# One layer kernel: keys laid out in runs of four, expert weights in one transfer, and loads moved in the fill and the drain

## The reference, cut to what matters

```
xn   = layernorm(x)
cq, ckv, kr0 = xn@Wc+bc, xn@Wckv+bckv, xn@Wkr+bkr        # 128, 128, 256 wide
q    = [cq@Wcq+bcq , cq@Wqr+bqr]  per head               # 16 heads, 32 + 16 wide
k    = [ckv@Wck+bck, kr0]         per head ; v = ckv@Wv+bv
attn = softmax over the 16 heads of one token (q_i . k_j), then attn @ v
x    = x + layernorm(attn_out@Wo + bo)
xf   = layernorm(x)
scores = softmax(xf@gate.T) ; top 6 of 64 experts, up to 128 rows each
routed = sum over chosen experts of  (silu(g)*u)@down * weight ; [g,u] = xf@gate_up[e]   # 192 each
shared = (silu(xf@G.T) * (xf@U.T)) @ D.T                 # 384 wide
x    = x + layernorm(routed + shared)
```

## Time and profile before

| what | us |
| --- | --- |
| median of 3 runs | 1913.72 (1912.94 to 1927.52) |
| the profiled execution's own time | 1907.77 |
| its span, first to last instruction | 1906.0 |
| tokens, start to about | 1325 |
| experts, about | 1330 to 1715 |
| norm, about | 1715 to 1906 |

### The profile page before, as it was taken

One profiled execution on the slowest core, in us unless ns is written; L12 is line 12 of the kernel. 1 busy time (PEld: TensorE's weight loads), 2 busy tenths in 40 slices (PEclk: granted clock), 3 DMA queues, 4 the chain that ended last, 5 costly groups with the idle time before them and its releaser, 6 DMA issues. The chain is left out here.

```text
span 1906.0 us, 48898 instructions
## 1 busy us (share of the span) xinstructions
PE 1769.8 (93%) x14281; PEld 1418.7 (74%) x14281; DVE 1509.3 (79%) x3940; ACT 967.3 (51%) x2129; POOL 522.6 (27%) x773
## 2 busy tenths in 40 slices
PE   5799999999999999999999999965999999998986
PEld 4688888888888888888888888854545555556865
DVE  6699999999999999999999999964444445437977
ACT  4465666666666656565656565631222323323433
POOL 1021211212121212121212121111344444444767
PEclk8799999999999999999999999977999999999998
DMA  6356565656666665656665666565799999988996
GB/s 223 89 140 174 146 177 147 173 154 166 161 160 168 157 171 153 175 152 174 153 173 154 174 153 176 133 160 168 235 312 324 336 330 346 349 258 320 416 414 265
DMA packets 549276, 400.83 MB, mean 210 GB/s; under 512 B 424872, under 2 KB 433192, under 8 KB 549160
## 3 DMA queue, kind: packets, MB, share of 16 engines
q1 hardware_dynamic: 528672, 341.77, 60.0%
q0 software_dynamic: 14336, 35.66, 7.7%
q10 hardware_dynamic: 6208, 22.68, 3.2%
HBM read 249.24 MB, written 150.63 MB: 210 GB/s over the span
## 5 line engine op out<-in xcount | busy, mean ns | idle before, releaser
L942 POOL TENSOR_SCALAR ve<-mv 128x1 f32<-128x1 f32 x192 | 42.3, 220 | 920.3 <-DVE mv L759 920.3
L646 ACT COPY kT<-bank 48x256 f32<-48x256 f32 x384 | 231.4, 603 | 37.2 <-PE bank L465 29.4
L1158 PE MATMUL e_gu<-w,xgT 128*128 128x384 f32 x512 | 187.6, 511 | 12.0 <-DMA w<-w_ed 9.8
L646 ACT COPY qT<-bank 48x256 f32<-48x256 f32 x512 | 188.5, 368 | 12.9 <-PE bank L465 2.0
L472 PE MATMUL bank<-wgu,xfT 128*128 128x416 f32 x512 | 188.8, 369 | 5.9 <-ACT xfT L646 4.9
L473 PE MATMUL bank<-wgu,xfT 128*128 128x416 f32 x512 | 183.6, 359 | 0.0
L1323 DVE SCALAR_TENSOR_TENSOR tanh<-tanh,e_gu 128x192 f32<-128x192 f32 x64 | 22.7, 355 | 165.0 <-ACT tanh L1246 165.0
L1158 PEld LDWEIGHTS e_gu<-w,xgT 128*128 128x128 f32 x512 | 94.5, 194 | 70.5 <-issue 10.7
L1424 POOL DMA_INDIRECT acc_scratch<-eo,sidx x64 | 101.5, 1587 | 120.0 <-ACT eo L1242 102.9
L1181 PE MATMUL e_ps<-w,hidT 96*128 96x512 f32 x256 | 128.2, 624 | 1.5 <-ACT hidT L1234 0.9
L476 PE MATMUL bank<-wgu,xfT 128*128 128x416 f32 x512 | 120.8, 359 | 0.3 <-DVE xfT L768 0.3
(11 more groups left out here) (184 smaller groups left out, 4750.4 us busy)
## 6 DMA issues: line engine op xcount, KB each, us to landing
w<-w_eg SPq DMA_DIRECT2D x60, 768.0 KB
acc_scratch<-zero SPq DMA_DIRECT2D x130, 256.0 KB, 4.0
w<-w_ed SPq DMA_DIRECT2D x60, 384.0 KB
w<-acc_scratch SPq DMA_DIRECT2D x40, 512.0 KB, 14.5
xf_scratch<-xf SPq DMA_DIRECT2D x64, 288.0 KB, 2.1
xin<-x SPq DMA_DIRECT2D x64, 256.0 KB, 2.8
x_raw<-xt SPq DMA_DIRECT2D x64, 256.0 KB, 3.2
v_scratch<-v SPq DMA_DIRECT2D x64, 256.0 KB, 3.5
```

Source lines behind the costliest of these rows:

```text
L646: nc.scalar.copy(dst, src).then_inc(done.sem, 1)
L1158: last = nc.tensor.matmul(gu_ps[par], xgT[:, par, n, :], w1[:, place, n, :], start=(n == 0), stop=(n == KD - 1))
```

## The change

- Keys: `kT` gets the layout of `qT` (`p c h t`), all 8 copies for it are ACT's, DVE's 2 are gone with their semaphore. The scores' columns now run head by head, so `prob` is laid out `n h t`, and DVE's two maxima read the scores with a step of 4 elements (`by_key`). The order of `v` in its DRAM copy follows: 4 stores in pieces of 128 bytes take the place of one, and SP issues them right behind the next tile's inputs.
- Fill: the low parts of `wo` and of the first two parts of `wgu` (parts 7 to 12) are POOL's; four bias loads go one iteration earlier.
- SP and the drain: the accumulators are cleared three iterations earlier (`i-2`), the bulk of the ranks is read back at iteration 64, the first experts' weights are issued in iterations 66 and 67.
- Experts: an expert's weights are one array of 128 rows by 2304 elements, in one transfer. The down product's first 128 features are a full product, cut in two halves of 256 columns; the other 64 features stand on partitions 0 to 63 and, again, on 64 to 127, and each half of the columns takes one of them. For that the hidden rows have 256 columns, of which the last 64 are written by a second DVE instruction. Gathered and hidden rows are turned from contiguous columns. The two small matmuls that find rows are one.

```diff
-        kT = kT_all[:, 0:P // 2 * H].rearrange("p (t h) -> p t h", h=H)
-        prob = sb("prob", [P, NBLK, B4, H])
+        kT = kT_all[:, 0:P // 2 * H].rearrange("p (c h t) -> p c h t", h=H, t=B4)
+        prob = sb("prob", [P, NBLK, H, B4])
...
+                if active(i - 1):
+                    sp.wait_ge(d_v.sem, d_v.at(i - 1))
+                    sp.wait_ge(v_in[1 - par].sem, v_in[1 - par].at(i - 3))
+                    settle(sp)
+                    dst = v_d[1 - par].rearrange("c (j t d) -> t c j d", t=B4, d=DH)
+                    for n in range(B4):
+                        sp.dma_start(dst[n], v[n:P:B4, :].rearrange("p (j d) -> p j d", d=DH)).then_inc(v_out.sem, 16)
...
-                if active(i - 5):
+                if active(i - 2):
                     for a in acc_d:
-                        sp.dma_start(rows(a, i - 5), zero[:, 0:D]).then_inc(acc_out.sem, 16)
+                        sp.dma_start(rows(a, i - 2), zero[:, 0:D]).then_inc(acc_out.sem, 16)
...
-                    sp.dma_start(v_d[1 - par], v[:]).then_inc(v_out.sem, 16)
...
-                if isinstance(i, int) and i == NT + 2:
+                if isinstance(i, int) and i == NT:
...
                     pe.wait_ge(a_kT.sem, a_kT.at(i - 2))
-                    pe.wait_ge(d_kT.sem, d_kT.at(i - 2))
...
-                    spread(by_token, b3, a_kT, 1, (0,))
+                    spread(kT, b3, a_kT, 1)
...
+                if isinstance(i, int) and i == NT + 2:
+                    act.wait_ge(pe_k.sem, pe_k.at(NT - 1))
+                    settle(act)
+                    for n in range(2):
+                        load_expert(act, n, n)
...
+                if isinstance(i, int) and i == NT + 3:
+                    for n in range(2, NW):
+                        load_expert(act, n, n)
...
-                if isinstance(i, int) and 0 <= i - NT - 1 < 2:
-                    act.wait_ge(pe_k.sem, pe_k.at(NT - 1))
-                    settle(act)
-                    for e in range(2):
-                        load_expert(act, 2 * (i - NT - 1) + e, 2 * (i - NT - 1) + e)
...
-                    for half in range(2):
-                        nc.vector.tensor_copy(by_token[64 * half:64 * half + DQ, 1, 4:8], sv[:, half]).then_inc(d_kT.sem, 1)
...
+                by_key = score_ps[:].rearrange("p (n h t) -> p n t h", n=NBLK, t=B4)
...
-                    nc.vector.tensor_reduce(smax4[:, halves[0]], sp4[:, halves[0]], AX.X, ALU.max).then_inc(d_s.sem, 1)
+                    nc.vector.tensor_reduce(smax4[:, halves[0]], by_key[:, halves[0]], AX.X, ALU.max).then_inc(d_s.sem, 1)
...
-                    pool.wait_ge(part_lo, 11)
+                    for n in ON_POOL:
+                        stage, w, m, _ = parts[n]
+                        pool.wait_ge(part_hi, n + 1)
+                        nc.gpsimd.tensor_tensor(w[:, 1, m, :], stage, w[:, 0, m, :].bitcast(F32),
+                                                ALU.subtract).then_inc(pool_lo, 1)
+                    pool.wait_ge(pool_lo, KD)
...
+            src = w_e[e * P:(e + 1) * P, :] if isinstance(e, int) else w_e[bass.ts(e, P), :]
+            sp.dma_start(w[:, place], src).then_inc(w_in[place].sem, 16)
...
+                    down = w[:, (place - 1) % NW, WU:WU + D]
                     for n in range(2):
-                        last = nc.tensor.matmul(out_ps, hidT[:, n, :], w2[0:PI, (place - 1) % NW, n, :],
-                                                start=(n == 0), stop=(n == 1))
+                        nc.tensor.matmul(out_ps[:, n], hidT[:, 0, :], down[:, n * HD:(n + 1) * HD], start=True, stop=False)
+                    for n in range(2):
+                        half = slice(64 * n, 64 * n + 64)
+                        last = nc.tensor.matmul(out_ps[:, n], hidT[half, 1, :], w[half, (place - 1) % NW, WU + D:],
+                                                start=False, stop=True)
...
-                    nc.tensor.matmul(find_ps[par][:, 0:P], sel[:], of(rank, j + 4), start=True, stop=True)
-                    nc.tensor.matmul(find_ps[par][:, P:P + 3], sel[:], of(base, j + 4), start=True,
+                    nc.tensor.matmul(find_ps[par][:, 0:P + 3], sel[:], of(rank, j + 4)[:, 0:P + 3], start=True,
...
+                    for a, b, at in ((0, I, 0), (P, I, I)):
+                        nc.vector.scalar_tensor_tensor(hid[:, par, at:at + b - a], tanh[:, par, a:b], gate[:, par:par + 1],
+                                                       gu_ps[par][:, I + a:I + b], ALU.mult, ALU.mult).then_inc(ed_h.sem, 1)
```

More of the change, by code:

```diff
@@ L60 @@
 BIG = 1.0e30
-PI = I // 2
+HD = D // 2
+WU = KD * 2 * I
+WE = WU + D + HD
 NW = 4
@@ L83, in constants, with by_partition @@
     return c
+def by_partition(w_gu, w_d):
+    n, k, m = w_gu.shape
+    up = w_gu.reshape(n, KD, P, m).transpose(0, 2, 1, 3).reshape(n, P, KD * m)
+    rest = w_d[:, P:].reshape(n, I - P, 2, HD).transpose(0, 2, 1, 3).reshape(n, P, HD)
+    return np.concatenate([up, w_d[:, 0:P], rest], 2).reshape(n * P, WE)
 def by_feature(x):
@@ L252, in token_pipeline @@
         PART_AT = [-1] * 4 + [0] * 9 + [1] * 2
+        ON_POOL = range(7, 13)
         consts_in = sem("consts_in")
@@ L648, in iteration, with spread @@
             def iteration(i, par):
-                def spread(dst, src, done, n, pair=range(2)):
-                    for a in pair:
+                def spread(to, src, done, n):
+                    dst = to.rearrange("p c (m a) t -> p a m c t", a=2)
+                    for a in range(2):
                         sv = src[64 * a:64 * a + DQ, :].rearrange("p (m r c t) -> p r m c t", m=4, r=2, t=B4)
@@ L654, in spread @@
                             copy(dst[64 * r:64 * r + DQ, a, 4 * n:4 * n + 4], sv[:, r], done)
-                if isinstance(i, int) and i == 0:
-                    for dst, src in ((bq, b_q), (bck, b_ck), (bv, b_v), (bo, b_o)):
-                        act.dma_start(dst[:], src.partition_broadcast(P)).then_inc(biases_in, 16)
                 if isinstance(i, int) and i >= 0 and i in PART_AT:
@@ L709, in iteration @@
                     copy(xT[:, 0].rearrange("p k t -> p (k t)"), x_raw[:, 1 - par, :], a_xT)
+                if isinstance(i, int) and i == -1:
+                    for dst, src in ((bq, b_q), (bck, b_ck), (bv, b_v), (bo, b_o)):
+                        act.dma_start(dst[:], src.partition_broadcast(P)).then_inc(biases_in, 16)
                 if isinstance(i, int) and i < 0:
@@ L747, in split @@
                 for n, (stage, w, m, _) in enumerate(parts):
-                    if PART_AT[n] == i:
+                    if PART_AT[n] == i and n not in ON_POOL:
                         dve.wait_ge(part_hi, n + 1)
@@ L995, in experts_and_norm @@
         tanh = sb("tanh", [P, 2, I])
-        hid = sb("hid", [P, 2, I])
-        hidT = sb("hidT", [PI, 2, P])
+        hid = sb("hid", [P, 2, 2 * P])
+        hidT = sb("hidT", [P, 2, P])
         eo = sb("eo", [P, NW, D])
@@ L1157, in iteration @@
                     for n in range(KD):
-                        last = nc.tensor.matmul(gu_ps[par], xgT[:, par, n, :], w1[:, place, n, :],
+                        last = nc.tensor.matmul(gu_ps[par], xgT[:, par, n, :], w[:, place, n * 2 * I:(n + 1) * 2 * I],
                                                 start=(n == 0), stop=(n == KD - 1))
@@ L1164, in iteration @@
                     for n in range(2):
[L1165 to L1167 removed]
+                        last = nc.tensor.transpose(hidT_ps[:, n * P:(n + 1) * P], hid[:, 1 - par, n * P:(n + 1) * P], ident)
                     last.then_inc(e_hT.sem, 1)
@@ L1241, in iteration @@
                     act.wait_ge(added[1 - par].sem, added[1 - par].at(j - 1 - NW))
-                    nc.scalar.copy(eo[:, (place - 1) % NW, :], out_ps).then_inc(ea_out.sem, 1)
+                    nc.scalar.copy(eo[:, (place - 1) % NW, :].rearrange("p (n d) -> p n d", n=2), out_ps).then_inc(ea_out.sem, 1)
                 if active(j):
```

98 lines of the change are left out of this document (39 added, 59 removed).

## The result

| | before | after |
| --- | --- | --- |
| median, us | 1913.33 (4 runs) | 1850.80 (4 runs, 1848.49 to 1854.52) |
| profiled execution, its span | 1907.77, 1906.0 | 1852.58, 1850.8 |

The account below looks back on a forecast made before the run. PE was taken to set the token stage's pace, PE and full DMA engines together the expert stage's. Terms -20 (keys), -5 (fill), -11 (drain), -5 (experts) sum to -41: 1907.8 - 41 + 5.9 = 1872.7, stated as 1872, range 1860 to 1884.

Parts of the forecast that it names:

- Key copies: Token loop: kT copies at 368 ns, no DVE copy, scores 0.25 us behind the last query matmul; 0.72 us per pair, 20 us.
- its slack of 0.5 us: Token loop: `oin` lands about 724.0 against a use at 724.60; slack shrinks to 0.5 us in the slow tile but holds.
- Maxima: DVE's maxima reading the scores in PSUM at a step of 4 cost 0 more, staying at 684 ns.
- rival (a): Token loop: strided maxima cost 0.47 us more each, a loss of 15 us, giving 1888; chance 0.17.
- (b): Token loop: strided maxima dearer still, making the kernel slower; at 1.0 us more each, 81 us and 1953; chance 0.07.
- (d): Token loop gets no faster, since another wait (`oin` or DVE) takes the keys' place: 1892; chance 0.08.
- `v` in pieces: Token loop: four transfers keep SP 2.6 us where one did, but are covered; cost 0.
- Fill: Start of the kernel: fewer DVE subtractions, earlier biases and quicker key copies in the first tiles; -5 us (0 to -10).
- Drain: Iterations after the token loop: moved loads shorten the `o` chain by 5.1 us and the `xf` stall by 7; -11 us.
- The chain of 9.8 us: Drain: `o` to `oin` without weights in the way takes 2.6 + 2.3 + 2.6 + 2.3 us, ending 5.1 us sooner.
- Experts: Expert stage: PE's list falls from 5.60 to 5.25 us, but DMA bytes stay, so only the last 7 experts gain; -5 us.
- Rival (c): Expert stage follows PE, through fuller transfers or a queue less full than it looks: -22 for -5, 1855; chance 0.10.

Follow-up runs that it names:

- a_again: The changed kernel run once more, unchanged: 1855.20 us, ratio 0.9691 to the kernel before; 314.9 us for 58 experts.
- a_drain: The changed kernel with the loads around the drain (first experts' weights, ranks, clearing) put back to their old places: ratio 0.9707 to the kernel before, drain stretch 106.8 us.
- a_drain2: The changed kernel with the loads around the drain put back, run a second time for the spread: ratio 0.9731 to the kernel before, drain stretch 111.3 us.
- b_keys: The kernel before with the new key layout alone (keys, maxima at step 4, v in four pieces): ratio 0.9877; 52 tiles in 981.1 us, 58 experts in 360.8.
- b_wide: The kernel before with its down weights' transfer on 128 partitions of 3072 bytes instead of 96 of 4096: ratio 0.9887, 58 experts in 326.0 us.
- x_two: The changed kernel with an expert's weights in two transfers on all 128 partitions (rows of 6144 and 3072 bytes) instead of one: ratio 0.9669, 58 experts in 315.1 us.
- c_128: The changed kernel with weights in two transfers, the second of 128 rows of 4096 bytes, 1.31 MB per expert instead of 1.18: 58 experts in 332.8 us.
- x_half: The changed kernel loading only the first half of each partition's weight row from expert 4 on: 58 experts in 306.6 us, against 316.3.
- x_full: The changed kernel with the down product's second part in full height instead of two row halves: 1863.07 us, ratio 0.9718 to the kernel before, 58 experts in 326.4 us.
- x_96: The changed kernel with the old weight transfers (128 rows of 6144 bytes, 96 of 4096): 1891.54 us, ratio 0.9848 to the kernel before, 58 experts in 356.2 us.
- p_low: The changed kernel with weights in two transfers, the second of 64 rows of 4096 bytes on partitions 0 to 63: 1883.15 us, 58 experts in 342.9 us.

## Why the prediction was right and wrong

**Key copies: right.** A pair takes 37.69 us (median of 24 pairs) for 38.41, the 0.72 of the forecast, by the mechanism named: distance 0.26, kT copies 367 ns. The 28 pairs gave less than the sum, 16.1 us in 26 pairs for 18.7, since some pairs are late for another cause: `oin`. I wrote that its slack of 0.5 us holds; in 12 of 57 tiles it did not, and cost up to 2.0 us. The slack was smaller than I had it, since I took the 2.3 us of the store's row for the load, which takes 2.5 in the page of the kernel before. No edit can be charged with these waits: from 230 to 1180 us they are 3.9 us in the changed kernel, 6.0 in a_again, 2.3 in the kernel before, but also 1.1 and 10.3 us in two executions of one kernel (a_drain and a_drain2), whose 52 tiles took 980.5 and 988.3 us.

**Maxima: right.** 688 and 681 ns for about 684. The rule of the Trainium skill (Advanced Engine Details and Errata, PSUM Cachelines), which I named beside rival (a), does not show in DVE's read at a step of four; it is stated of matmuls. Rivals (a) and (b) are out, and so is (d), since the token loop did get faster. **`v` in pieces: right** within b_keys' 981.1 us.

**Fill: size right, cause mostly wrong.** It gave 3.2 us in the two profiles and 5 over all of them, but by the quicker key copies, which I had named last; POOL's part and the biases gave nothing measurable.

**Drain: right way, too large.** 7 to 8 us by medians and 4.5 by the mean of all profiles, for 11. The chain of 9.8 us took 9.03, but PE's waits for `oin` did not shrink in sum: two of 5.47 and 5.30 us stand where one of 10.61 stood. What shrank are DVE's waits for a store of `xf`, from 15.1 us in the drain to 6.2: one of the two fell to 1.19 us, near the 1 of the forecast, the other only to 5.00.

**Experts: wrong, and this is the failed step.** I wrote "the bytes stay: 344 GB/s x 5.60 us = 1.93 MB" and held 344 GB/s as a ceiling, since the share was 1.05; and "one transfer for two moves the same bytes; 0". Both terms failed.

The 344 GB/s was read where PE idled 2.5 of 149 us. It was the rate at which PE's list asked for weights, so multiplying it by 5.60 us and dividing by it again had to give 5.60. The share says how long engines were busy, not at what rate: b_wide moves 349 GB/s under the old list, x_two 361 and c_128 364, all at 1.04 or 1.05. An estimate from these: at 364 GB/s the 1.93 MB of the sum take 5.30 us, and the 1.97 MB that the trace of the changed kernel has for an expert take 5.41, against PE's new list of 5.27. So the bytes still bind, but little: 10 us by x_half.

Nor was the form of the transfer free. In the kernel before, the part on 96 partitions stretched rows beside it (0.256 us for 0.237 per 6144 bytes in the mean), and where weights came late PE lost the wait and then clock. What I priced at 0 is worth 22 us alone (b_wide). PE's shorter list is worth 10 (x_full against after), but only with it: x_96, with that list on the old transfers, took 356.2 us, and the old list on them 339.8, 345.1 and 360.8. Rival (c) happened, by "a queue that was less full than it looks"; the sign against a ceiling that I noted, 319 and 344 GB/s at one share, deserved more than 0.10.

**The sum** by ratios: keys 23.5, transfer 22, PE's list 10, drain 7, fill 0: 62 us for the 63 measured. The intervals of these terms reach 5 to 12 us to either side, so the agreement is luck in part. For the keys, 17.7 us in b_keys' 52 tiles and 5.3 before them agree; its profile as a whole is only 7.7 us shorter, since its expert stage, which the layout does not touch, was 21 us longer.

## What to carry to other kernels

A busy share of the DMA engines near 1 is no bandwidth limit: divide bytes by time in two stretches, and if the rate differs, ask what stretches the rows before holding it as a ceiling. A rate that is read where the compute engine hardly waits is what that engine asks for. Here loads that ran beside others did best on all 128 partitions, and on 32 to 95 far better than on 0 to 63. Where two bounds lie on each other, a shorter list and a better transfer must be costed together, and one profile of a stretch with DMA races in it does not tell 5 us.

## What the runs showed of the hardware

- 64 rows of 4096 bytes beside 128 rows of 6144: 342.9 us for 58 experts on partitions 0 to 63, 310.3 on 32 to 95. The transfers beside them suffer too (6144-byte rows at 0.267 and 0.249 us in the mean).
- At a busy share of 1.01 to 1.05 the DMA engines moved 306 (p_low) to 368 GB/s (a_drain2) over the same 260 us.
- Products on two row halves of the array start 6 or 7 ns apart and together take the time of one product of their columns: the down product takes 1.60 us for 1.92, and PE's list 5.27 us where x_full, without the halves, has 5.61.
- A wait of 4.15 us on PE was followed by a stretch of granted clock 0.60, and the product after it took 5.48 us for 2.85.
- A reduction on DVE that reads PSUM at a step of four elements costs what a contiguous one costs, 681 to 688 ns for 512 elements; a copy that writes in runs of four costs 367 ns for 256 elements where one that writes single elements costs 602.
